# Seventeen instead of 21 weight slabs rounded in the expert steps, and eight of the later 19 by GpSimd in place of VectorE

## The reference, cut to what matters

```python
def _layernorm(x): return (x - m) / jnp.sqrt(v + 1e-5)          # over the last axis, 512
# x: (4, 512, 512) = 2048 tokens; ctx_2048: (4, 512, 512), one matrix W[e] for each of 4 experts
h = _layernorm(x)
e = jnp.minimum(token_id // 6250, 3)                            # expert of each token
y = (silu(h @ W[e].T) * (h @ W[e].T)) @ W[e].T                  # the same matrix three times
x = x + tanh(g_xattn) * y
h = _layernorm(x)
gate = silu((h @ fp8(gate_w)) * gate_scale)                     # gate_w, up_w: 512 x 1536
up = (h @ fp8(up_w)) * up_scale
x = x + tanh(g_ffn) * ((gate * up) @ fp8(down_w)) * down_scale  # down_w: 1536 x 512
```

## Time and profile before

| | us |
|---|---|
| median of three runs | 401.18 |
| lowest and highest | 400.94, 401.9 |
| the profiled execution | 401.0 |
| its span in the profile | 399.3 |
| busy in the span: PE | 378.4 (95%) |
| DVE | 224.1 (56%) |
| ACT | 185.5 (46%) |
| POOL | 163.2 (41%) |

### The profile page before, as it was taken

The page is one execution under the profiler, slowest core; times in us unless marked ns, Lnnn a source line. Parts: engine busy times, 40 slices in busy tenths (PEclk is TensorE's granted clock), DMA queues, the critical chain, the costliest instruction groups (busy, mean ns, idle before and its releaser), DMA issues.

```text
span 399.3 us, 6082 instructions
## 1 busy us (share of the span) xinstructions
PE 378.4 (95%) x1920; PEld 184.3 (46%) x1920; DVE 224.1 (56%) x467; ACT 185.5 (46%) x297; POOL 163.2 (41%) x204
## 2 busy tenths in 40 slices
PE   3889899999999999999999999999999999999992
PEld 2444455555545544444444444444444444444460
DVE  5878979998787696787434222224222225322253
ACT  3779457789778428693432222222222222222220
POOL 4778889999999831411008000006200004400003
PEclk9999999999999999999999999999999999999997
DMA  7698684354445340760002000001100000200002
GB/s 263 190 313 183 127 214 113 88 108 114 101 115 112 80 105 2 178 167 0 0 2 79 28 0 0 2 0 54 53 0 0 0 0 28 79 0 2 0 0 105
DMA packets 40075, 29.99 MB, mean 75 GB/s; under 512 B 31192, under 2 KB 31216, under 8 KB 40048
## 3 DMA queue, kind: packets, MB, share of 16 engines
q1 hardware_dynamic: 37488, 21.26, 21.4%
q0 software_dynamic: 2560, 8.39, 6.1%
HBM read 18.11 MB, written 4.19 MB: 56 GB/s over the span
## 4 chain that ended last, share of the span: by engine, by line
PE 79%; DVE 10%; ACT 3%; issue 3%; POOL 2%; DMA 1%; SPq 1%; DVEq 0%; ACTq 0%; POOLq 0%
PE bank L1551 36%; PE bank L1565 17%; PE bank L1467 11%; PE bank L1483 7%; PE bank L1391 3%; PE bank L1487 3%; PE bank L1425 1%; DMA X<-x2rows 1%; DVE xs L1112 1%; DVE stats L1062 1%; DVE W L1278 1%; DVE xs L1372 1%; DVE row_hot L997 1%; DVE X L1369 1%; DVE cs L1289 1%
## 5 line engine op out<-in xcount | busy, mean ns | idle before, releaser
L1551 PE MATMUL bank<-X,W 128*128 (+1 forms) x752 | 170.0, 379 | 0.1
L1551 PEld LDWEIGHTS bank<-X,W 128*128 128x128 bf16 x752 | 73.5, 98 | 88.8 <-ACT late_norms L879 0.6
L1289 DVE SCALAR_TENSOR_TENSOR cs<-bank,up_mul,cs 128x512 f32<-128x512 f32 x47 | 35.3, 751 | 107.1 <-PE bank L1551 102.4
L1565 PE MATMUL bank<-W,cs 128*128 128x512 bf16 x376 | 89.0, 379 | 0.5 <-ACT W L762 0.5
L837 ACT ACTIVATE cs<-bank,gate_mul 128x512 f32<-128x512 f32 x47 | 32.2, 684 | 75.5 <-PE bank L1551 75.5
L844 ACT ACTIVATE cs<-cs 128x512 f16<-128x512 f32 x47 | 29.5, 628 | 79.8 <-DVE cs L1289 79.7
L676 POOL TENSOR_TENSOR xs<-xs,X 128x512 f32<-128x512 f32 x12 | 15.3, 1275 | 125.2 <-DVE X L1369 124.9
L1565 PEld LDWEIGHTS bank<-W,cs 128*128 128x128 f16 x376 | 36.6, 98 | 44.0 <-issue 0.5
L1467 PE MATMUL bank<-M,X 128*128 (+1 forms) x228 | 52.5, 379 | 2.1 <-ACT X L728 1.5
L1315 DVE TENSOR_TENSOR cs<-cs 128x512 f16<-128x512 f32 x47 | 33.7, 716 | 31.4 <-ACT cs L844 31.4
L1483 PE MATMUL bank<-M,hTh 128*128 (+1 forms) x152 | 35.9, 378 | 1.6 <-DVE xs L1112 1.6
(11 more groups left out here) (172 smaller groups left out, 385.6 us busy)
## 6 DMA issues: line engine op xcount, KB each, us to landing
ws<-in_L_ffn_gate_w SPq DMA_DIRECT2D x12, 256.0 KB, 2.6
ws<-in_L_ffn_up_w SPq DMA_DIRECT2D x12, 256.0 KB, 3.2
ws<-in_L_ffn_down_w SPq DMA_DIRECT2D x12, 256.0 KB, 2.9
cs<-in_ctx SPq DMA_DIRECT2D x2, 1024.0 KB, 6.7
X<-in_ctx SPq DMA_DIRECT2D x2, 1024.0 KB
xs<-in_x,order POOLq DMA_INDIRECT x16, 4.2
dsc<-in_L_ffn_down_scale SPq DMA_DIRECT2D x1, 256.0 KB
X<-x2rows SPq DMA_TRANSPOSE x16, 3.1
```

Of the source, the lines that this page charges most:

```text
L1289: v.scalar_tensor_tensor(out=fuse[:, c % 2, :], in0=UP[c % 2][:], scalar=up_mul[:, c:c + 1], in1=sg[:, c % 2, :], op0=ALU.mult, op1=ALU.mu ...
L1551: ins = t_.matmul(dst[c % 2][:].rearrange("p (t i) -> p t i", t=TPG), w, x2_group(g, part, k), start=(k == 0 and part == 0), stop=(k == KC ...
L1565: ins = t_.matmul(ACC[t][:], fuse_part(g, c, part)[:, t * P:(t + 1) * P], W8[:, down_slab(c), :], start=(c == 0 and part == 0), stop=(c == ...
```

## The change

Seventeen slabs instead of 21 are rounded in the steps; the doubled steps are 8 and 12 instead of 7, 9, 12, 14 and 16, and step 17 rounds none. The other 19 are rounded in group 0, in units of four, three, three, three, two, two and two slabs. Of these, eight slabs of down (d1 to d5, d7, d9, d11) are rounded by GpSimd: VectorE clamps `w_big`, GpSimd adds into `ws` in place and subtracts. The other eleven stay with VectorE. The norms of g0 and g1 move from the steps to group 0, and so late norms begin at unit 4 in place of 5. Two new semaphores count GpSimd's late slabs, and a load whose slot held such a slab waits until it has been rounded.

```diff
-    EARLY = 21
-    EARLY_NORMS = 18
-    LATE_ORDER = ("g2", "d3", "g3", "d4", "g4", "g5", "d5", "g6", "g7", "d6", "d7", "d8", "d9", "d10", "d11")
-    TURNS = {25: 11, 27: 12, 29: 13, 31: 14, 33: 15}
+    EARLY = 17
+    EARLY_NORMS = 16
+    LATE_UNITS = (("g0", "d1", "g1", "d2"), ("g2", "d3", "g3"), ("g4", "d4", "g5"), ("g6", "d5", "g7"), ("d6", "d7"),
+                  ("d8", "d9"), ("d10", "d11"))
+    LATE_ORDER = [name for unit in LATE_UNITS for name in unit]
+    LATE_POOL = ("d1", "d2", "d3", "d4", "d5", "d7", "d9", "d11")
+    TURNS = {21: 11, 24: 12, 27: 13, 30: 14, 33: 15}
...
-            return 0 if lo < 2 or lo >= STEPS - 1 else 2 if lo in (7, 9, 12, 14, 16) else 1
+            return 0 if lo < 2 or lo >= STEPS - 2 else 2 if lo in (8, 12) else 1
...
+        def slab_summed(engine, n):
+            if by_pool(n):
+                engine.wait_ge(late_q, pool_turn(n))
+            else:
+                engine.wait_ge(sum_done, own_turn(n))
...
+            def round_late(name):
+                n = EARLY + LATE_ORDER.index(name)
+                pool.wait_ge(big_done, EARLY + pool_turn(n))
+                row = ws[:, slab_slot(n)]
+                g.tensor_tensor(row, row, w_big[:, slab_slot(n)], ALU.add).then_inc(late_s, 1)
+                pool.wait_ge(late_s, pool_turn(n))
+                g.tensor_tensor(W8[:, n, :], row, w_big[:, slab_slot(n)], ALU.subtract).then_inc(late_q, 1)
...
             x2_low(TILES - 5)
-            for i in range(3):
-                ln_scalars(STEPS + STATS1_LEAD + i, (STEPS + i) % 2, 1, 2)
-            for i in range(4):
-                x2_low(TILES - 4 + i)
+            round_late("d1")
+            ln_scalars(STEPS + STATS1_LEAD, STEPS % 2, 1, 2)
+            round_late("d2")
...
+            x2_low(TILES - 1)
+            round_late("d7")
+            round_late("d9")
             ffn_norm(1, 2 * KC, IC)
+            round_late("d11")
...
+            def late_own(slabs):
+                for n in slabs:
+                    if not by_pool(n):
+                        late_sum(n)
+                        late_round(n)
+            def late_big(slabs):
+                for n in slabs:
+                    if by_pool(n):
+                        slab_big(n, slab_slot(n))
...
             ffn_scales(0, 0, 2)
-            late_sum(EARLY)
+            late_big(late_slabs(0))
             add_expert(STEPS - 2)
-            late_round(EARLY)
-            late_sum(EARLY + 1)
-            late_round(EARLY + 1)
             late_stats(0)
+            late_own(late_slabs(0))
             unit_fuse(0, 0)
...
                     unit_fuse(g, c)
                     if first:
-                        late_sum(EARLY + 2 * c - 2)
+                        late_big(late_slabs(c - 1))
+                        late_own(late_slabs(c - 1)[:1])
                     unit_low(g, c)
                     if first:
-                        late_round(EARLY + 2 * c - 2)
-                        late_sum(EARLY + 2 * c - 1)
-                        late_round(EARLY + 2 * c - 1)
+                        late_own(late_slabs(c - 1)[1:])
```

More of the change, by code:

```diff
@@ L361, in down_slab, with late_slabs, by_pool, pool_turn @@
             return EARLY_NORMS + c if EARLY_NORMS + c < EARLY else EARLY + LATE_ORDER.index(f"d{c}")
+        def late_slabs(c):
+            first = EARLY + sum(len(unit) for unit in LATE_UNITS[:c])
+            return range(first, first + len(LATE_UNITS[c])) if c < len(LATE_UNITS) else ()
+        def by_pool(n):
+            return n >= EARLY and LATE_ORDER[n - EARLY] in LATE_POOL
+        def pool_turn(n):
+            return sum(by_pool(m) for m in range(n + 1))
+        def own_turn(n):
+            return n + 1 - pool_turn(n)
+        def slab_summed(engine, n):
[3 more added lines that the diff above has]
+                engine.wait_ge(sum_done, own_turn(n))
+        def slab_rounded(engine, n):
+            if by_pool(n):
+                engine.wait_ge(late_q, pool_turn(n))
+            else:
+                engine.wait_ge(q_done, own_turn(n))
         def walk_words(engine):
@@ L862, in late_abs @@
             def late_abs(c):
-                for n in range(EARLY + 2 * c, min(EARLY + 2 * c + 2, SLABS)):
+                for n in late_slabs(c):
                     slab_abs(n, slab_slot(n), slab_turn(n), slab_before(n))
             def late_second(c):
-                if 4 <= c < 7:
+                if 3 <= c < 7:
                     for i in range(2):
[L871 to L874, removed]
+                        n = gu_slab(2, 2 * (c - 3) + i)
+                        slab_square(n, i, EARLY_NORMS + 2 * (c - 3) + i)
+                scale_down(c)
             def late_norm(c):
-                act.wait_ge(norm_done, EARLY_NORMS + 2 * (c - 4))
+                act.wait_ge(norm_done, EARLY_NORMS + 2 * (c - 3))
                 a.activation(late_norms[:, 2 * KC * (c - 4):2 * KC * (c - 3)], GATE[(c + 1) % 2][:, 0:2 * KC],
@@ L895, in group @@
                     gate_silu(g, c)
-                    if first and 5 <= c < 8:
+                    if first and 4 <= c < 8:
                         late_norm(c)
@@ L1265, in late_sum @@
             def late_sum(n):
[L1267 to L1272, removed]
-            def late_round(n):
[L1276 to L1279, removed]
+                slot = slab_slot(n)
+                dve.wait_ge(abs_done, n + 1)
+                dve.wait_ge(q_done, own_turn(n) - 1)
+                v.scalar_tensor_tensor(out=w_sum[:], in0=w_big[:, slot], scalar=FP8_FLOOR, in1=ws[:, slot],
+                                       op0=ALU.max, op1=ALU.add).then_inc(sum_done, 1)
+            def late_round(n):
+                dve.wait_ge(sum_done, own_turn(n))
+                v.scalar_tensor_tensor(out=W8[:, n, :], in0=w_big[:, slab_slot(n)], scalar=FP8_FLOOR, in1=w_sum[:],
+                                       op0=ALU.max, op1=ALU.subtract, reverse1=True).then_inc(q_done, 1)
+            def late_own(slabs):
[5 more added lines that the diff above has]
+                for n in slabs:
+                    if by_pool(n):
+                        slab_big(n, slab_slot(n))
             def unit_fuse(g, c):
@@ L1539, in late_norms_of @@
                 for i in range(2):
-                    norms(gu_slab(2, 2 + 2 * (c - 5) + i), EARLY_NORMS + 2 * (c - 5) + i, i, GATE[(c + 1) % 2], i * KC)
+                    norms(gu_slab(2, 2 * (c - 4) + i), EARLY_NORMS + 2 * (c - 4) + i, i, GATE[(c + 1) % 2], i * KC)
             def gate_or_up(g, c, which):
@@ L1555, in gate_up @@
             def gate_up(g, c):
-                if isinstance(g, int) and g == 0 and 6 <= c < 9:
-                    pe.wait_ge(norm_read, c - 5)
+                if isinstance(g, int) and g == 0 and 5 <= c < 9:
+                    pe.wait_ge(norm_read, c - 4)
                 gate_or_up(g, c, 0)
```

22 lines of the change are left out of this document (15 added, 7 removed).

## The result

| | before | after |
|---|---|---|
| median of four runs each, us | 401.54 | 409.43 |
| lowest and highest | 400.94, 402.21 | 408.86, 410.64 |
| ratio, 95% interval | | 1.020 (1.017 to 1.023) |
| the profiled execution, and its span | 401.0, 399.3 | 408.86, 407.1 |
| busy in the span: PE, DVE | 378.4, 224.1 | 380.1, 229.8 |

A forecast was written before the change was run, and what follows sets the result against it. TensorE was taken to be full, leaving only about 2.0 us of waits to win. Waits of 10.3 us in place of 1.67 add 8.6, less 0.2 in the steps: 401.0 + 8.4 = 409.4 us, range 403.5 to 413.5.

The forecast's parts named there:

- the price of a hold: First group: GpSimd and VectorE take turns, each waiting for the other's whole instruction; most hits cost 1.0 to 1.2 us.
- the 1.1 that was named as the sign: First group: VectorE's round and low half lines would have means over 1.1 us if the forecast was right.
- Unit by unit: TensorE's waits ahead of the last expert product and downs 1 to 5 and 8, summing to 10.3 us.
- The 115 ns: Skill page's delay after the other engine's end; by it the sum would be 2 to 3 us higher; rows preferred.
- Unit 4: First group: g5 held by d4's round and x2_low; low 4 ends at 176.1, due at 173.3: 2.8 us lost.
- The square term: Unit 4: waits for the squares of slabs that come late themselves, counted inside the 2.8 us.
- Unit 8: Ahead of fuse 8: d11's two GpSimd instructions hold f_scale, up_mul and f_inv up to 2.4 us; 1.0 lost.
- The steps: Steps before the group: four slabs fewer gain 0.2 us, bounds 0 to 0.3; a like collision can come at 8 and 12.
- One hold for a slab: Rival, first group: VectorE gets between GpSimd's sum and round, 8 instructions held instead of 16; 405.1 us, chance 0.17.
- Hidden: Rival, first group: VectorE is held but spare time covers it, waits stay at 1.7 us; 400.8 us, chance 0.08.
- Faster: Rival: holds hit GpSimd only, VectorE has 2.2 us less, the 1.05 us wait goes; 399.3 us, chance 0.08.
- Worse: Rival: unit 8 waits 2.8 us instead of 1.0, units 6 and 7 do not catch up; 413 us, chance 0.07.

The follow-up runs named there:

- one-column: Changed kernel with GpSimd's sixteen late rounding instructions cut to one column of 512 each, all waits and order kept: 401.54 us, ratio 0.9995.
- the fill runs: Changed kernel with each of GpSimd's sixteen late instructions replaced by two fills that only write the same rows: 401.65 us, ratio 0.9989.
- the run with dummy matmuls: Changed kernel with six unused matmuls of 256 columns ahead of each of down 2 to 5: 409.75 us, ratio 1.0203 against before.
- the form with 21 slabs in the steps: Kernel before, its rounding schedule and norms kept, but six of its fifteen late slabs rounded by GpSimd: 402.89 us, ratio 1.0027.
- the one with the clamp behind: Changed kernel with the clamps for GpSimd's slabs put behind the low half, not ahead of VectorE's first sum: 409.6 us, ratio 1.0193.

## Why the prediction was right

**The bound and the price of a hold** came out as stated: TensorE full but for its waits, VectorE's instruction ending 0.55 us behind GpSimd's. The one-column and the fill runs show that nothing else of the change costs anything as long as VectorE has only eleven slabs, since both stand at before's time. The means of roundings and low halves in the group, 1.45 and 1.28 us, are over the 1.1 that was named as the sign.

**Unit by unit**, predicted against measured wait: last expert product 0.5 / 0.69, unit 1 0.65 / 0.75, unit 2 1.6 / 1.52, unit 3 2.0 / 2.06, unit 4 2.8 / 1.11, unit 5 1.7 / 1.72, unit 8 1.0 / 0. The layout's times of the low halves hold to 0.1 us: low 2 ends at 160.39 (160.5 predicted), low 4 at 176.03 (176.1). The 115 ns that the prediction set against the rows stand in the Trainium skill (SBUF — State Buffer, "A bandwidth-pool intuition that's wrong (but worth ruling out)") for a DMA whose descriptors wait for a VectorE instruction, which is another pair; going by the rows was right.

**Unit 4.** The wait was mis-sized (1.11 us, under the 1.5 that was named as the least) and the cost was not. TensorE was at half clock from about 168.9 to 172.4, within the 2.42 us from down 3 to the gate and up matmuls and the 4.46 us behind them; the same distances of unit 2 and 3 are 1.74 and 3.45 us, so 1.7 us went there (2.42 - 1.74 + 4.46 - 3.45). 1.11 + 1.7 = 2.8, the term. The prediction did not foresee the clock, nor did it need to: the run with dummy matmuls kept the clock and started down 4 at the same time. So down 4 waited for VectorE at either clock, and the slower clock only hid a part of that wait. The square term inside the 2.8 was not seen as a wait in the kernel after, because TensorE came late itself; with the clock kept, 0.2 us and one more small wait of it show.

**Unit 8 is the term that failed.** f_scale was held as said (compare the last of the earlier trace rows), its two small followers were not:

```profile
194.75 1.28 POOL L666 TENSOR_TENSOR ws<-ws,w_big 128x512 f32<-128x512 f32 x1
194.83 1.23 DVE L1198 TENSOR_SCALAR f_scale<-f_top 128x4 int32<-128x4 int32 x1 [1.47 <-POOL f_top L674]
...
196.09 0.16 DVE L1201 TENSOR_TENSOR up_mul<-up_mul,f_scale 128x4 f32<-128x4 f32 x1
196.11 1.28 POOL L668 TENSOR_TENSOR W<-ws,w_big 128x512 bf16<-128x512 f32 x1
196.17 0.17 DVE L1202 RECIPROCAL f_inv<-f_scale 128x4 f32<-128x4 f32 x1
...
198.96 1.24 PE L1623 MATMUL bank<-W,cs 128*128 128x512 bf16 x5
```

Between GpSimd's two instructions stands a semaphore. L1201 starts at 196.09, 0.02 us ahead of L668, and L1202 runs beside it unheld. One hold of 1.1 us was within the spare time, but only just: low half 8 ends at 198.75, and the matmuls ahead of down 8 are issued by 198.95. A second hold would have shown for about 0.9 us.

**The steps** were forecast to win 0.2 and lost about 0.3: TensorE is busy 79.01 us in place of 79.34, with one wait of 0.63 at 84.3 us for two of 0.29 and 0.15. The doubled step kept GpSimd until 82.1, so that the low half of a tile's rows (L680 at 82.08) met a clamp, which took 1.38 us at 82.14, and the add behind it came late. The like collision that the prediction thought possible came, and it turned the gain into a loss.

**The sum**: 0.69 + 0.75 + 1.52 + 2.06 + 2.8 + 1.72 = 9.5, less 1.7, with 0.3 in the steps 8.1, against 7.8 of span and 7.9 between the medians; 0.3 us is not found, within what records missing from a trace leave open. The forecast total of 8.4 was 0.5 too high beside the profiled executions, and 0.3 beside these terms: unit 8's 1.0, less 0.5 in the steps and 0.3 in the first two waits. That the median still came out at 409.43 beside a forecast of 409.4 is luck. The 8.4 were added to before's profiled execution of 401.0, while its median in the result is 401.54; one execution beside the other, the profiled ones are 7.9 apart.

**The rivals.** One hold for a slab (405.1) falls: both of GpSimd's instructions are held (medians 1.65 and 1.60), and both hold. Hidden (400.8) is what the form with 21 slabs in the steps comes near to, with 402.89 against 402.12; it fails here for want of spare time, not of mechanism. Faster falls with it; its 1.05 us was to be had, but by moving one GpSimd instruction whose result ScalarE waited for. The rule named there (Trainium skill, Perfetto Trace Analysis, "Optimizing Scalar/DVE Operations"), by which such a move might not help, was right in its sign and short of the size. Worse falls with unit 8.

## What to carry to other kernels

GpSimd's idle time is not room for work that reads SBUF while VectorE runs instructions with two operands in SBUF: count a moved slab as its own time on the old engine, once for each meeting, and ask how much spare time each unit has for it. Lay such a stretch out in order, with every row's end, because holds cost nothing up to the spare time and full price beyond it. And look at the kernel as it stands for a GpSimd instruction that others wait for and that stands behind one with a late input.

## What the runs showed of the hardware

TensorE's clock was at half for 3.4 us in the middle of the kernel after, not at its start or end (stretches: length, busy of PE, PEld, DVE, ACT, POOL, clock, DMA, GB/s):

```profile
165.40:168.90 3.50, 1.58 (x15) 0.85 (x14) 3.50 (x3) 2.63 (x5) 3.42 (x3) 1.00 0.58 97
168.90:172.36 3.46, 3.46 (x10) 1.18 (x8) 3.43 (x5) 1.56 (x3) 1.84 (x3) 0.51 0.79 241
```

In the stretch ahead of it TensorE had been busy 1.58 of 3.50 us; in the second it was busy throughout, at 1.2 in place of 2.4 GHz. The kernel with dummy matmuls, busy 2.00 us of the first stretch, kept 1.00 in the second; the one with the clamp behind has the same dip, 0.50 from 176.2 to 179.6. Both times it fell within 2 us behind the end of one of the group's long waits, but not behind each of them: after the wait of 1.72 us that ends at 183.20 in the kernel after it stayed full. There the dip cost 1.7 us of TensorE's time, which were hidden because TensorE would have waited for VectorE anyway; what it cost with the clamp behind was not tried.

A small VectorE instruction can start between two GpSimd instructions and is then not held: the 0.16 us of L1201 at 196.09, where one GpSimd row ends at 196.03 and the next starts at 196.11. L1202, which reads one operand, started inside the next one and was not held either, while f_scale and the clamps, which read one operand too, were (1.23 us at 194.83, 1.38 at 82.14). The runs do not sort out which small instructions are held.
